# Conditional convolution and routed linear layer on one core: tiles 2 and 3 take the paired form of the convolution, and VectorE's order in a step is changed up to step 12

## The reference

```python
ffn_in = conv1d(x, weight, 9 taps, 4 groups, pad 4) + (cond @ c_weight.T)[:, :, None] + bias
base = ffn_in @ base_W.T + base_b                     # 512 -> 512
logits = ffn_in @ router_W.T + router_b               # 512 -> 15
topk_p, topk_i = top_k(softmax(logits), 8)
w = einsum('btk,btke->bte', topk_p, onehot(expert_map[topk_i]))
h = einsum('btd,erd->bter', ffn_in, A)                # 8 experts, rank 16
out = x + base + einsum('bter,eor->bto', h * w[..., None], B) * 2.0
```

## Time and profile before

| | |
|---|---|
| median of 3 executions | 185.14 us (184.2 to 185.57) |
| profiled execution, its own time | 184.44 us |
| its span, first to last instruction | 182.6 us |
| TensorE matmul busy | 178.4 us (98%) |
| TensorE weight loads busy | 171.1 us (94%) |
| VectorE busy | 150.8 us (83%) |
| GpSimd busy | 139.8 us (77%) |
| ScalarE busy | 81.2 us (44%) |

### The profile page before, as it was taken

One profiled execution on the slowest core, in us unless ns is written; L12 is line 12 of the kernel. 1 busy time (PEld: TensorE's weight loads), 2 busy tenths in 40 slices (PEclk: granted clock), 3 DMA queues, 4 the chain that ended last, 5 costly groups with the idle time before them and its releaser, 6 DMA issues.

```text
span 182.6 us, 3930 instructions
## 1 busy us (share of the span) xinstructions
PE 178.4 (98%) x1236; PEld 171.1 (94%) x1236; DVE 150.8 (83%) x509; ACT 81.2 (44%) x247; POOL 139.8 (77%) x139
## 2 busy tenths in 40 slices
PE   7999999999999999999999999999999999999993
PEld 3687999999999999999999999999999999999992
DVE  0597888898888889888888988889898889978673
ACT  3648743354544434454443445454344444422320
POOL 2118999999888898888889888888988887885620
PEclk9999999999999999999999999999999999999999
DMA  6999751757475553646565454656445721233304
GB/s 172 348 388 340 252 178 14 243 199 204 152 233 174 173 181 124 178 152 230 159 198 174 135 170 154 228 178 210 175 106 201 230 78 63 97 115 115 118 0 172
DMA packets 17876, 32.01 MB, mean 175 GB/s; under 512 B 1984, under 2 KB 3136, under 8 KB 17856
## 3 DMA queue, kind: packets, MB, share of 16 engines
q1 hardware_dynamic: 17424, 31.40, 53.1%
q10 hardware_dynamic: 432, 0.36, 0.6%
HBM read 23.36 MB, written 8.39 MB: 174 GB/s over the span
## 4 chain that ended last, share of the span: by engine, by line
PE 96%; DVE 2%; issue 0%; POOL 0%; DVEq 0%; POOLq 0%
PE wide_ps L606 62%; PE wide_ps L648 12%; PE conv_banks L592 11%; PE edge_bank L592 3%; PE conv_banks L606 2%; PE odd_bank L635 2%; PE wide_ps L554 2%; PE conv_banks L663 1%; PE conv_banks L565 1%; PE conv_banks L563 1%; DVE xr L966 1%; DVE y L856 0%; DVE y_rows L774 0%; PE edge_bank L621 0%; DVE y_hi L891 0%
## 5 line engine op out<-in xcount | busy, mean ns | idle before, releaser
L606 PE MATMUL wide_ps<-wide_hi,y_hi 128*128 128x400 f32 (+1 forms) x248 | 66.0, 326 | 0.1
L606 PE MATMUL wide_ps<-wide_hi,y_lo 128*128 128x400 f32 (+1 forms) x248 | 62.6, 313 | 0.0
L606 PE MATMUL wide_ps<-wide_lo,y_hi 128*128 128x400 f32 (+1 forms) x248 | 62.5, 313 | 0.0
L486 POOL TENSOR_TENSOR terms_lo<-terms,terms_hi 128x512 fp32r<-128x512 f32 x28 | 36.3, 1298 | 18.4 <-ACT terms_hi L385 18.4
L606 PEld LDWEIGHTS wide_ps<-wide_hi,y_hi 128*128 128x128 f32 x248 | 44.0, 188 | 2.5 <-issue 0.5
L606 PEld LDWEIGHTS wide_ps<-wide_lo,y_hi 128*128 128x128 f32 x248 | 45.9, 188 | 0.0
L606 PEld LDWEIGHTS wide_ps<-wide_hi,y_lo 128*128 128x128 f32 x248 | 45.9, 188 | 0.0
L504 POOL TENSOR_TENSOR y_lo<-y,y_hi 128x512 fp32r<-128x512 f32 x31 | 40.3, 1299 | 5.7 <-ACT y_hi L400 5.7
L481 POOL TENSOR_TENSOR xr<-xr,base_b_sb 128x512 f32<-128x512 f32 x32 | 41.7, 1302 | 0.0
L407 ACT ACTIVATE hw_hi<-odd_bank 128x128 fp32r<-128x128 f32 x31 | 8.6, 278 | 54.3 <-PE odd_bank L635 54.3
L768 DVE TENSOR_TENSOR xr<-wide_ps,xr 128x512 f32<-128x512 f32 x30 | 20.7, 691 | 5.2 <-PE wide_ps L648 3.8
(11 more groups left out here) (90 smaller groups left out, 308.4 us busy)
## 6 DMA issues: line engine op xcount, KB each, us to landing
xr<-x_rows SPq DMA_DIRECT2D x32, 256.0 KB, 3.6
out<-xr SPq DMA_DIRECT2D x31, 256.0 KB, 3.2
terms<-x_units SPq DMA_DIRECT2D x28, 256.0 KB, 2.9
edges<-x_edges SPq DMA_DIRECT2D x14, 256.0 KB, 3.1
wide_sb<-wide_w SPq DMA_DIRECT2D x4, 328.0 KB, 4.9
x_in<-x_first SPq DMA_DIRECT2D x3, 264.0 KB, 4.7
weights_sb<-conv_w SPq DMA_DIRECT2D x2, 192.0 KB, 5.3
x_in<-x_first SPq DMA_DIRECT2D x2, 132.0 KB, 2.8
```

Of the source, the lines that this page charges most:

```text
L486: nc.gpsimd.tensor_tensor(terms_lo[i % 2][:, :, :, :], terms[i][:, :, :, :], terms_hi[i % 2][:, :, :, :].bitcast(F32), ALU.subtract)\
L606: mm = nc.tensor.matmul(sums_of(t, k)[:, b, 0:columns[1] - columns[0]], a[k % 2][:, r, :], w[:, r, columns[0]:columns[1]], start=r == 0 an ...
```

## The change

1. **Tiles 2 and 3 in paired form, in float32.** `conv_first` stays for tiles 0 and 1. For tiles 2 and 3 `conv_whole` issues one float32 matmul over 256 columns for each block: shared and own for both tiles, and for tile 2 an edge block too (three and two matmuls, where there were two of 512 columns for each). `x_in` has two buffers fewer; `first_terms`, `first_edges` are loaded instead.
2. **Differences for them.** GpSimd subtracts `first_terms[0]` and `first_edges` in SBUF, after VectorE's last `wide_lo`; VectorE subtracts `first_terms[1]` in SBUF, behind `mark(0, 0)`.
3. **VectorE conditions tiles 2 and 3 by three additions** each (`condition` of two, and `reach`, the third, split off as a function of its own).
4. **Order of the start.** ScalarE makes the condition of groups 2 and 3 ahead of `conv_high(1)`; GpSimd's `bias_rows(0)` stands ahead of `edge_low` and `bias_rows(1)` ahead of `terms_low(5)`; on VectorE `add_out(0)` leads step 1 and `turn(3)` ends it. The convolution's weights are regrouped (12 blocks in place of 14), and their pieces are loaded in another order.
5. **Order of steps 2 to 11.** VectorE: `condition` (two additions), `hw_low`, `choose`, `best`, `reach`, `add_out`, `mark`, `difference`, `weigh`, `turn`. ScalarE: `hw_hi` ahead of `y_hi`. From step 12 both are as before.
6. In `conv` TensorE waits for `y_rows_ready` of tile t-1 only ahead of the edge block.

```diff
+FIRST = 2
+LATE = 12
...
             load_conv(2)
-            load_x(2)
+            load_first_terms(0)
             sync.wait_ge(wide_in[0], 16)
+            sync.dma_start(first_edges[:, :, :, :], x_edges[0]).then_inc(first_edges_in, 16)
+            load_conv(4)
+            sync.wait_ge(wide_in[1], 16)
             load_conv(3)
-            load_x(3)
+            load_first_terms(1)
...
+            def conv_whole(t):
+                i, h = t - FIRST, t % 2
                 pe.wait_ge(y_rows_ready, t - 1)
+                pe.wait_ge(conv_w_in[2 + i], 16)
+                pe.wait_ge(first_terms_in[i], 16)
+                nc.tensor.matmul(conv_ps[:, h, 0, :, :], conv_sb[:, W_SUM[t], :],
+                                 first_terms[i][:, 1, :, :], start=True, stop=True)
+                pe.wait_ge(first_difference[i], 1)
+                mm = nc.tensor.matmul(conv_ps[:, h, 1, :, :], conv_sb[:, W_OWN[t], :],
+                                      first_terms[i][:, 0, :, :], start=True, stop=True)
+                if h == 0:
+                    pe.wait_ge(cond_biased, GROUPS)
+                    pe.wait_ge(first_edge_ready, 1)
+                    mm = nc.tensor.matmul(edge_ps, conv_sb[:, W_QUARTERS[t // 2], :],
+                                          first_edges[:, 0, :, :], start=True, stop=True)
+                mm.then_inc(conv_done, 1)
...
             conv_low(0)
+            pool.wait_ge(wide_lo_ready, RUNS)
+            pool.wait_ge(first_terms_in[0], 16)
+            nc.gpsimd.tensor_tensor(first_terms[0][:, 0, :, :], first_terms[0][:, 0, :, :],
+                                    first_terms[0][:, 1, :, :], ALU.subtract)\
+                .then_inc(first_difference[0], 1)
...
                 if up_to_tile(t, TILES - 3):
                     condition(t + 2, (k + 2) % GROUPS, q + (k + 2) // GROUPS)
-                    turn(t + 2, k + 2)
-                    hw_low(t - 1, k - 1)
-                elif t == TILES - 2:
+                    if from_tile(t, LATE):
+                        reach(t + 2, (k + 2) % GROUPS)
+                        turn(t + 2, k + 2)
+                if up_to_tile(t, TILES - 2):
                     hw_low(t - 1, k - 1)
...
+                choose(t, k)
+                dve.wait_ge(logits_ready, t + 1)
+                if from_tile(t, LATE) and up_to_tile(t, TILES - 5):
+                    difference(t + 4, k)
+                best(t, k)
+                if not from_tile(t, LATE):
+                    reach(t + 2, (k + 2) % GROUPS)
+                dve.wait_ge(top_ready, t + 1)
+                if up_to_tile(t, TILES - 3):
+                    add_out(t - 1, (k - 1) % UNROLL)
+                mark(t, k)
+                if not from_tile(t, LATE):
+                    difference(t + 4, k)
+                weigh(t, k)
+                if not from_tile(t, LATE):
+                    turn(t + 2, k + 2)
```

More of the change, by code:

```diff
@@ L100, in build @@
         zero_exp = sb("zero_exp", [P, 1])
-        x_in = [sb(f"x_in{i}", [P, Q, BLKI]) for i in range(START)]
+        x_in = [sb(f"x_in{i}", [P, Q, BLKI]) for i in range(FIRST)]
+        first_terms = [sb(f"first_terms{i}", [P, 2, Q, MK]) for i in range(START - FIRST)]
+        first_edges = sb("first_edges", [P, 2, Q, MK])
         terms = [sb(f"terms{i}", [P, 2, Q, MK]) for i in range(URING)]
@@ L416, in _ @@
             bias_condition(range(1, 2), 2)
+            bias_condition(range(2, GROUPS), 3)
             conv_high(1)
@@ L421, in _ @@
             exponentials(0, 0)
-            bias_condition(range(2, GROUPS), 3)
             terms_high(START, 0)
@@ L433, in step @@
                     return
[L434 removed]
+                if from_tile(t, LATE) and up_to_tile(t, TILES - 2):
                     y_high(t + 1, k + 1)
@@ L786, in condition @@
                 rows = y_rows[h]
-                reached = slice(EDGE, P) if h == 0 else slice(0, EDGE)
                 dve.wait_ge(conv_done, t + 1)
@@ L792, in condition, with reach @@
                     .then_inc(common_ready, 1)
-                dve.wait_ge(common_ready, t - START + 1)
+                dve.wait_ge(common_ready, t - FIRST + 1)
                 nc.vector.tensor_tensor(rows[:, :, other, :], conv_ps[:, h, 1, :, :],
                                         rows[:, :, shared, :], ALU.add).then_inc(own_ready, 1)
-                dve.wait_ge(own_ready, t - START + 1)
+            def reach(t, g):
+                h = g % 2
+                shared = 1 - h
+                rows = y_rows[h]
+                reached = slice(EDGE, P) if h == 0 else slice(0, EDGE)
+                dve.wait_ge(own_ready, t - FIRST + 1)
                 nc.vector.tensor_tensor(rows[reached, :, shared, :], edge_ps[reached],
@@ L909, in step @@
                 if t == 0:
-                    condition_first(2)
+                    condition(2, 2, 0)
+                    reach(2, 2)
                     turn(2, 2)
+                    hw_low(0, 0)
                     choose(1, 1)
@@ L914, in step @@
                     best(1, 1)
+                    condition(3, 3, 0)
+                    reach(3, 3)
+                    return
+                if t == 1:
+                    add_out(0, 0)
                     dve.wait_ge(top_ready, 2)
                     mark(1, 1)
-                    condition_first(3)
-                    hw_low(0, 0)
-                    return
-                if t == 1:
+                    difference(START + 1, 1)
+                    weigh(1, 1)
                     turn(3, 3)
-                    difference(START + 1, 1)
-                    add_out(0, 0)
-                    weigh(1, 1)
                     return
@@ L945, in step @@
                     return
-                if up_to_tile(t, TILES - 2):
-                    choose(t, k)
-                    dve.wait_ge(logits_ready, t + 1)
-                    if up_to_tile(t, TILES - 5):
-                        difference(t + 4, k)
-                    best(t, k)
-                    dve.wait_ge(top_ready, t + 1)
-                    if up_to_tile(t, TILES - 3):
-                        add_out(t - 1, (k - 1) % UNROLL)
-                    mark(t, k)
-                    weigh(t, k)
+                choose(t, k)
[12 more added lines that the diff above has]
+                weigh(t, k)
+                if not from_tile(t, LATE):
+                    turn(t + 2, k + 2)
             steps_of(step)
```

72 lines of the change are left out of this document (38 added, 34 removed).

## The result

| | before | changed |
|---|---|---|
| median | 185.11 us (22 executions beside it) | 185.62 us (185.19 to 186.41, 22) |
| ratio | | 1.0042, 95% interval [1.0029, 1.0056] |
| profiled execution, its span | 184.44, 182.63 us | 186.41, 184.61 us |

The interval of the ratio excludes 1, so this is slower, by 0.78 us (0.54 to 1.04) going by the ratio, while the two medians lie 0.51 apart; it is within the 1% about which the prediction spoke. Four executions that took 292.75 to 998.06 us, the profiled one of e8 among them, are left out of the ratios and give no rows. The page of the changed kernel: span, busy times, clock in 40 slices, the chain that ended last.

The account below looks back on a forecast made before the run. TensorE bounds the kernel (96% of the chain). Span 182.6 - 0.55 (start) + 0.51 (step 12) = 182.56, with 1.84 outside 184.4, -0.04 against the profiled execution; median 185.14 becomes 185.1 us, range 183.8 to 186.0.

Parts of the forecast that it names:

- the start's gain: Up to step 2: of 1.29 us of removed TensorE matmuls, 0.55 us survives the waits of the start.
- the loss at step 12: At the order's change back, two transposes stand ahead of `hw_lo(11)`, which comes late: 0.51 us lost, once.
- the subtraction of `first_terms[1]` taken at nothing: VectorE's new subtraction at the start takes 0.42 us but is covered, so it costs nothing.
- a late operand priced at 0.10: At tile 1's front bank, a late operand adds 0.10 us, as at the third product of `up` in step 26.
- The start's order of waits: TensorE waits for `y_hi`, `up_lo`, then the edge block's `edge_lo`; kept gain falls from 1.13 to 0.74 to 0.55 us.
- one of the prediction's signs of being wrong: At the start: the prediction is wrong if VectorE's `first_terms` subtraction is long or late while GpSimd works; no size given.
- a rival with a chance of 0.17: At the start, VectorE's new subtraction and GpSimd hold each other up: 185.5 us mild, 186.6 hard; chance 0.17, hard 0.05.
- its mild one: The rival's mild form at the start: GpSimd 0.42 us late, step 2 at 21.7, 0.13 kept, 185.5 us.
- The 185.5 that the prediction gave by that rule: At the start, VectorE and GpSimd exclude each other in SBUF for a whole instruction: at least the mild form, 185.5 us.
- VectorE, tied to `add_out`: Before step 12, VectorE's `add_out` waits for TensorE's `up`, starting 4.03 us into a step; `hw_lo(11)` starts 3.57 into step 12.
- Steps 2 to 11 cost nothing: In the new order added waits make nobody late; TensorE keeps its 5.49 us and shorter steps: no cost, no gain.
- the forecast's own -0.04: Whole profiled execution: 184.4 us forecast against 184.44 before; the difference of -0.04 is added to the median of 185.14.

Follow-up runs that it names:

- e8: Changed kernel with the transpose and `reach` moved to just behind `hw_lo` in steps 2 to 11, and shared buffers at their old addresses: 185.06 us, 1.0011.
- e4: Changed kernel without VectorE's subtraction of `first_terms[1]`, so tile 3 is computed from another operand: 185.33 us, 1.0021.
- e17: e16 with VectorE's subtraction reading its second operand from PSUM, copied there by ScalarE behind `conv_high(1)`: 184.52 us, 0.9966.
- e5: Kernel before with the new order in steps 2 to 5, 8 to 11, 14 to 17 and 20 to 23: 186.51 us, 1.0098.
- e6: Changed kernel with `reach` and the transpose of tile t+2 in the step's front part, the transpose behind `hw_lo`, in steps 2 to 11: 185.47 us, 1.0030.
- e7: Changed kernel with gaps in SBUF so that every buffer both kernels share lies at its address of before: 185.32 us, 1.0026.
- e9: Changed kernel with 24 small writes at the head of VectorE's program: 185.48 us, 1.0033.
- e10: Kernel before with 24 small writes at the head of VectorE's program: 184.64 us, 0.9982.
- e1: Kernel before with only the new order of VectorE and ScalarE in steps 2 to 11, its start untouched: 185.29 us, 1.0011.
- e13: Changed kernel with ScalarE copying one operand of VectorE's `first_terms[1]` subtraction to PSUM, ahead of the condition of groups 2 and 3: 186.26 us, 1.0073.
- e16: e8 with 24 small writes at the head of VectorE's program, the `first_terms[1]` subtraction left in SBUF: 184.94 us, 0.9983.

## Why the prediction was wrong

It forecast 185.1, the start's gain and the loss at step 12 cancelling: no change, where the kernel became slower by 0.78. Three of its terms failed: the subtraction of `first_terms[1]` taken at nothing (it cost 0.16), a late operand priced at 0.10 where it cost 0.28 at the edge block (0.16 with the rest of the start), and all behind step 2 but step 12 taken at nothing (0.46). The start step by step, each counted from the mark:

| kept at | prediction | changed | e4 |
|---|---|---|---|
| `turn_hw(0)` | 1.13 | 0.89 | 1.06 |
| `up(0)` | 0.74 | 0.57 | 0.74 |
| edge block of tile 4 | 0.55 | 0.30 | 0.48 |
| step 2 | 0.55 | 0.23 | 0.39 |

1. **The start's order of waits was right**: `y_hi(1)`, then `up_lo`, then the edge block, the gain shrinking at each. The step that failed is "The subtraction of `first_terms[1]`, 0.42 as `difference` is, I take at nothing". It took 0.81 and lengthened `y_lo(1)` by 0.18, and TensorE waited 0.29 for it in place of 0.10. e4 brings back 0.16. A subtraction that is long while GpSimd works was one of the prediction's signs of being wrong, and its price stood in a rival with a chance of 0.17, not in the sum. This is the rival of VectorE and GpSimd holding each other up, in a form half as strong as its mild one: GpSimd was 0.18 late, not 0.42. The Trainium skill's rule, cited there from "SBUF — State Buffer", named the right pair; its exclusion for a whole instruction fits VectorE roughly (0.81, ending 0.28 behind `conv_lo`), while `y_lo(1)` was held by less than a whole subtraction. The 185.5 that the prediction gave by that rule lies near what was measured by luck: it counts 0.42 for a hold that cost 0.16, and none of what stands under 2 and 4. With an operand in PSUM VectorE wasn't held (e17).
2. **The other 0.16 of the start is a price taken too low.** In e4, with no sharing, GpSimd is on time: `edge_lo` is done (`y_lo(2)` starts) 14.57 behind the mark, forecast 14.59. But the edge block starts 0.19 behind that, and step 2 another 0.44 later, 0.63 in all, where the forecast had the 0.10 of step 26 and the undisturbed 0.35. GpSimd, then TensorE, in e4:

```profile
20.62 0.74 POOL L515 TENSOR_TENSOR edge_lo<-edges,edge_hi 128x256 fp32r<-128x256 f32 x1
21.31 1.29 POOL L521 TENSOR_TENSOR y_lo<-y,y_hi 128x512 fp32r<-128x512 f32 x1
...
21.50 0.35 PE L613 MATMUL edge_bank<-edge_hi,conv_hi 128*128 128x256 f32 x1
...
21.94 0.90 PE L627 MATMUL wide_ps<-wide_hi,y_hi 128*128 128x400 f32 x4
```

The changed kernel has the same, 0.18 and 0.42.

3. **Step 12 was right**: 0.53 for 0.51, never won back, by the mechanism given (`hw_lo(11)` 3.54 us into the step for 3.57). e5 makes it four times 0.5, e6 removes it. "VectorE, tied to `add_out`", held.
4. **"Steps 2 to 11 cost nothing" was right of the order and incomplete.** The order itself costs nothing there (e5, between its returns). But the change moves two things that the prediction didn't weigh at all. It moves buffers, for 0.04 in every fourth distance, 0.28 in all (e7). And it moves the places where VectorE pauses, for 0.33 more up to `turn_hw(15)`, while the 0.15 that the kernel before lost to such a pause at step 26 went (e9, e10). Together 0.28 + 0.33 - 0.15 = 0.46, more than the start's error of 0.32. With the 0.02 at step 12 and the forecast's own -0.04 that makes +0.76; the two profiles have +0.79, the ratio +0.78 (0.54 to 1.04).
5. **Loads** were taken at nothing. In the changed kernel's profile, with its late mark, nothing waits for a load between the mark and step 2; in executions with an early mark waits for loads show (e1, e13 to e17). What they cost in the medians no profile tells.
6. A slip that changes no verdict: the range's upper end, "the mild form, and half the spread of the three runs", is 185.5 + 0.69 = 186.2, not 186.0.

What stays open: what VectorE waits for in its pauses and why it comes at some places only, which buffers make 5.15 of 5.11, why the first passes take from 1.6 to 2.9, and how much of e17's lead over e16 is the PSUM operand.

## What to carry to other kernels

Where one engine walks behind another with a few tenths in hand, the order of its queue may be changed, but not back: at the seam two long operations meet ahead of the one result that is waited for. When a change moves an already tuned kernel by half a per cent, compare the distances between one recurring instruction in both traces before explaining anything; here they laid open terms of 0.04 to 0.5, of which the diff suggests only the start and step 12. Check too that a price read at one wait holds at another: 0.10 at the third product of `up` was 0.28 at the edge block. A few idle instructions at the head of an engine's program are a cheap test of whether a pause belongs to the computation or to the place in the program.

## What the runs showed of the hardware

- A 128x256 subtraction of VectorE with both inputs in SBUF took 0.81 to 0.86 us beside GpSimd's subtractions, 0.42 with one input in PSUM; GpSimd's 128x512 took 1.47 for 1.29.
- A late operand cost 0.10 over the wait at the third product of `up`; at the edge block, from the end of `edge_lo` to the next step, 0.60 to 0.63 passed where 0.35 is the undisturbed time from the block on.
- VectorE pauses of 0.3 to 0.6 us (0.24 is usual ahead of `add_out`, 0.15 ahead of `hw`) without a cause in the semaphores, with packets of 8 KB on the instruction queue 0.9 to 1.4 us behind four of them; 24 small instructions ahead removed them in two kernels. With 12 the end of a third was 1.06 us longer.
- The same code with other SBUF addresses took 5.15 for 5.11 us in every fourth distance.
- The first six float32 passes over 256 columns took 1.58 to 2.93 us at a granted clock that reads 1.00, a pass every 0.43 or every 0.22; the profiles differ by up to 1.24 us at the mark behind them.
